# Dense products by column half, one cast behind each relu, row loads issued by GpSimd, and an early statistics record, in a three-layer graph network

## The chip, the cores and the metric

The kernel runs on one core of one Trainium2 chip. The metric is the device time of one execution in microseconds (us). PE is the matrix engine, DVE the vector engine, ACT the activation engine, POOL (GpSimd) issues indirect transfers, and SP issues most of the plain ones. ACT issues plain transfers too.

## The reference

A graph of 100,000 nodes with 128 values each and 25,000 edges, sorted by destination. The rows are normalised, three graph layers follow, each with a relu and a batch normalisation over all nodes, and the input is added.

```python
h = jnp.maximum(_layernorm(x, axis=-1), 0.0)
xn = _bn(h, g0, be0)
h = _bn(relu(_gcn_conv(xn, src, dst, edge_weight, W1, b1, n)), g1, be1)              # 128 -> 256
h = _bn(relu(_graph_conv(h, src, dst, edge_weight, Wrel2, brel2, Wroot2, n)), g2, be2)  # 256 -> 256
h = _bn(relu(_graph_conv(h, src, dst, edge_weight, Wrel3, brel3, Wroot3, n)), g3, be3)  # 256 -> 128
return x + h
# _graph_conv: segment_sum(ew[:, None] * x[src], dst) @ Wrel + brel + x @ Wroot
# _bn: g * (x - mean over all nodes) * rsqrt(var over all nodes + 1e-5) + b
```

## The kernel before

**Stages.** Setup, "norm", layers 1 to 3 (in the text l1, l2, l3) and "out", one behind the other, with a barrier between two. In a layer, two kinds of work share the engines. The *dense* work takes all nodes in 98 tiles of 1,024 columns (two column halves of 512), with channels on partitions. The *edge* work takes the edges in 49 chunks of 512, so two dense tiles go with one chunk. At a layer's end `fold` (line 1447) reads the batch statistics and folds scale and shift into the next weights. It aggregates, for each block of 128 channels, all 245 records that `bn_stats` left (two for each dense tile, one for each chunk), with one `bn_aggr` on DVE (line 1489). l1 and l2 have two blocks, l3 one.

**Dense work in l2 and l3** (`dense_layer`). Each f32 input is split: ACT casts it to a "top" part (`cast` in `tops`, line 1050), DVE subtracts that and leaves a "rest" part in place (`rests`, line 1078). PE then forms each product as three matmuls for each of two input blocks. A *unit* is one output block by one column half: 6 matmuls, then one relu on ACT (line 1037). A tile has `per` units, 4 in l2 and 2 in l3. Units alternate between two PSUM banks, so unit u+2 waits for the relu of unit u. Before a tile's first unit PE waits (`wait_use(pe, spl[j], i, kb * CH)`) until all four of its rests are done.

**What sets the order.** `pipeline` writes each engine's program as turns, one for each dense tile. A stage of lag L handles in turn t the tile t-L, so the lag says how many turns after its load a tile gets a step. The edge work has its steps in each second turn, ahead of the dense steps. I call the dense tile right behind edge work **A** and the next, which has no edge work ahead of it, **B**. A round is edge work, A, B. In l2 and l3 the dense stream starts slowly: its first 8 tiles come one in two turns, each right behind edge work. After these there are 45 rounds with an A and a B. The lags around the change are: casts and rests at `late` (8 tiles), products and relus at `ahead` = `late` + 2, and statistics one later. So before the change a tile's two halves are cast and split two turns ahead of its products.

**Edge work.** In l2 a chunk needs on ACT two relus of source rows (1371), two affines (1380), two copies of a product (1388), two "sum" casts (1415), and two casts of the destination inputs (`hd_top`, 1438, placed behind a dense tile's steps). In l2 DVE multiplies, scans (1309) and splits, and in l3 it multiplies and scans. The scan needs the chunk's same-node flags (`row_same`, 128 KB) and in l2 the weights (`row_weight`, 256 KB). ACT issues both transfers behind the affines (1351, 1353). POOL issues four gathers for each chunk (1170) once PE has turned the chunk two before.

## Time and profile before

| | us |
|---|---|
| median of 3 runs | 3771.5 (3755.3 to 3779.79) |
| the profiled execution, its own time | 3759.16 |
| its span in the trace | 3757.3 |
| PE busy | 2988.7 (80%) |
| DVE busy | 2613.1 (70%) |
| ACT busy | 2327.1 (62%) |
| POOL busy | 1348.4 (36%) |
| DMA, mean over the span | 304 GB/s |

The trace shows l1 until 1301 us, its fold until the first work of l2 at 1330, l2 until 2442, l3 from 2469 to 3219, and "out" behind it. A busy share is a mean over stages, so what bounds one stage is read from that stage's rows. The ends of matmuls are modelled: two matmuls that follow each other without a gap start 0.23 us apart although each is drawn 0.39 us long. So PE's lost time is read from the starts.

### The profile page before, as it was taken

What the parts mean: (1) busy time and instruction counts of PE and PEld (TensorE: products, weight loads), DVE (VectorE), ACT (ScalarE), POOL (GpSimd) and SP (SyncE); (2) the same over time, 40 slices, a digit from 0 to 9 for tenths busy, and PEclk for the clock granted to TensorE, in tenths of its full rate; (3) what the DMA queues carried; (4) which work ended last, traced back from release to release, by engine and by line L of the source; (5) the groups of instructions that cost most, each with busy time, mean ns of one, the idle gap of its engine ahead of it and who ended that gap; (6) DMA issues with size and microseconds to landing.
All of it is one profiled execution on the core that took longest, in us unless ns stands there. A gap on an engine that the chain in (4) does not pass through costs nothing. (4 is left out here: it accounts for less than half of the span.)

```text
span 3757.3 us, 52409 instructions
## 1 busy us (share of the span) xinstructions
PE 2988.7 (80%) x12445; PEld 2000.6 (53%) x12445; DVE 2613.1 (70%) x5586; ACT 2327.1 (62%) x4070; POOL 1348.4 (36%) x1194
## 2 busy tenths in 40 slices
PE   3565658988899769999999999959999999554543
PEld 3455534444444346777777777735555555333332
DVE  6576647877777858888888888757877777533332
ACT  4586736666666547877788778736666666333331
POOL 1444555545455232222222221022222321067475
PEclk9787879999999979999999999979999999655555
DMA  5586648888788769999999999769999999799997
GB/s 202 192 286 223 228 169 298 309 294 299 287 313 306 273 215 345 337 340 339 343 334 340 346 340 339 275 208 320 346 348 351 346 339 339 290 368 362 378 361 233
DMA packets 344639, 1142.11 MB, mean 304 GB/s; under 512 B 55625, under 2 KB 103266, under 8 KB 294386
## 3 DMA queue, kind: packets, MB, share of 16 engines
q1 hardware_dynamic: 221468, 933.98, 66.6%
q0 software_dynamic: 62656, 77.70, 12.2%
q10 hardware_dynamic: 60438, 129.60, 9.7%
q8 instruction: 24, 0.39, 0.0%
q14 instruction: 53, 0.43, 0.0%
HBM read 625.81 MB, written 515.28 MB: 304 GB/s over the span
## 5 line engine op out<-in xcount | busy, mean ns | idle before, releaser
L1170 POOL DMA_INDIRECT l_ed_gathered<-agg_rows,pos_cols x392 | 432.0, 1102 | 1462.7 <-PE l_ps L1182 704.0
L1078 DVE TENSOR_TENSOR l_dn_hi<-l_dn_hi,l_dn_top 128x512 fp32r<-128x512 f32 x784 | 501.5, 687 | 248.2 <-ACT l_dn_top L1050 228.0
L1023 PE MATMUL l_ps<-l_dn_top,wroot_top 128*128 128x512 f32 x1176 | 503.0, 428 | 85.9 <-ACT l_dn_ho L1037 43.3
L1037 ACT ACTIVATE l_dn_ho<-l_ps,bias_fold 128x512 f32<-128x512 f32 x588 | 395.8, 682 | 151.9 <-PE l_ps L1023 148.6
L1050 ACT ACTIVATE l_dn_top<-l_dn_hi 128x512 fp32r<-128x512 f32 x784 | 448.0, 623 | 65.2 <-DMA l_dn_hi<-h_dense 65.2
L1023 PE MATMUL l_ps<-l_dn_hi,wroot_top 128*128 128x512 f32 x1176 | 466.8, 397 | 0.0
L1023 PE MATMUL l_ps<-l_dn_top,wroot_rest 128*128 128x512 f32 x1176 | 466.4, 397 | 0.0
L685 PE MATMUL l_ps<-l_dn_columns,w_fold 128*128 128x512 f32 x784 | 391.3, 624 | 62.5 <-ACT l_dn_ho L720 55.6
L1608 POOL DMA_INDIRECT out<-out_rows_dst,out_cols x196 | 305.2, 1557 | 289.5 <-DMA out<-out_od_ot 189.6
L609 PE MATMUL norm_ln_ps<-norm_ln_ho 128*128 128x130 f32 x1568 | 248.3, 319 | 182.9 <-ACT norm_ln_ho L597 93.3
L597 ACT ACTIVATE norm_ln_ho<-norm_ln_x,norm_ln_nbias,norm_ln_rstd 128x128 f32<-128x128 f32 x784 | 303.8, 480 | 106.5 <-DVE norm_ln_nbias L550 102.8
L1067 DVE BATCH_NORM_STATS2 bn_stats_all<-l_dn_ho 128x512 f32 (+1 forms) x588 | 365.5, 678 | 2.0 <-ACT l_dn_ho L1037 2.0
L1629 PE MATMUL out_ps<-ident,out_od_hi 128*128 128x128 f32 x784 | 191.9, 426 | 189.6 <-ACT out_od_hi L1617 186.7
L609 PEld LDWEIGHTS norm_ln_ps<-norm_ln_ho 128*128 128x128 f32 x1568 | 228.1, 228 | 203.1 <-ACT norm_ln_ho L597 103.3
L1023 PEld LDWEIGHTS l_ps<-l_dn_top,wroot_top 128*128 128x128 f32 x1176 | 222.8, 189 | 201.1 <-issue 83.1
L798 POOL DMA_INDIRECT l_ed_src_rows<-h_rows,src_cols x196 | 213.0, 1087 | 310.8 <-PE l_ps L880 245.5
L720 ACT ACTIVATE l_dn_ho<-l_ps,bias_fold 128x512 f32<-128x512 f32 x392 | 261.4, 693 | 67.0 <-PE l_ps L685 42.4
L1645 DVE TENSOR_TENSOR out_od_ot<-out_ps,out_od_xt 128x512 f32<-128x512 f32 x196 | 135.5, 692 | 227.6 <-PE out_ps L1629 218.3
L639 POOL DMA_INDIRECT h_rows<-map_values,out_cols x196 | 190.2, 971 | 277.2 <-issue 202.1
L1629 PEld LDWEIGHTS out_ps<-ident,out_od_hi 128*128 128x128 f32 x784 | 153.1, 222 | 228.5 <-ACT out_od_hi L1617 169.8
L685 PEld LDWEIGHTS l_ps<-l_dn_columns,w_fold 128*128 128x128 f32 x784 | 135.8, 194 | 241.6 <-ACT l_dn_ho L720 146.3
L1617 ACT ACTIVATE out_od_hi<-out_od_hi,bn_shift,bn_scale 128x1024 f32<-128x1024 f32 x98 | 121.5, 1240 | 216.5 <-DMA out_od_hi<-h_dense 200.3
(233 smaller groups left out, 5900.2 us busy)
## 6 DMA issues: line engine op xcount, KB each, us to landing
h_dense<-l_dn_ho SPq DMA_DIRECT2D x196, 1024.0 KB, 10.2
l_dn_hi<-h_dense SPq DMA_DIRECT2D x196, 1024.0 KB
l_dn_rows<-h_rows SPq DMA_DIRECT2D x98, 520.0 KB
h_rows<-norm_ln_ho SPq DMA_DIRECT2D x97, 520.0 KB
h_dst<-l_ed_ho SPq DMA_DIRECT2D x98, 512.0 KB, 10.6
l_ed_hd<-h_dst ACTq DMA_DIRECT2D x98, 512.0 KB
h_dense<-l_dn_ho SPq DMA_DIRECT2D x98, 512.0 KB
out_od_hi<-h_dense SPq DMA_DIRECT2D x98, 512.0 KB
```

Source lines behind the costliest of these rows:

```text
L597: ins = act.activation(ho[:, j, g, 0:C], xt[:, j, g, :], ACT.Relu, bias=nb[:, j, g:g + 1], scale=rs[:, j, g:g + 1])
L609: ins = pe.matmul(ps[:, 0, 0:TC], ho[0:rows, j, g, 0:C], ho[0:rows, j, g, :], start=first and g == 0, stop=final and g == G - 1, skip_grou ...
L685: pe.matmul(ps[:, 2 + u % 2, 0:CW], wfold[1][:, 0, m * C:(m + 1) * C], hc[:, j % 2, c * CW:(c + 1) * CW], start=True, stop=True).then_inc( ...
L720: act.activation(ho[:, j, m, c * CW:(c + 1) * CW], ps[:, 2 + u % 2, 0:CW], ACT.Relu, bias=bfold[1][:, m:m + 1]).then_inc(rl[j], 1)
L1023: ins = pe.matmul(o, a, b, start=t == 0, stop=t == len(terms) - 1)
L1037: act.activation(ho[:, j, m, c * CW:(c + 1) * CW], ps[:, u % 2, 0:CW], ACT.Relu, bias=bf[:, m:m + 1]).then_inc(rl[j], 1)
L1050: act.activation(top[:, j % 2, k, cc], hi[:, j, k, cc], ACT.Copy).then_inc(tp[j], 1)
L1067: dve.bn_stats(stats[:, m, (i * NS + j) * CH + c, :], ho[:, j, m, c * CW:(c + 1) * CW]).then_inc(st[j], 1)
L1078: dve.tensor_tensor(rest[:, j, k, cc], hi[:, j, k, cc], top[:, j % 2, k, cc].bitcast(FP), ALU.subtract).then_inc(spl[j], 1)
L1170: pool.indirect_dma_start(tg[:, j, g, :], None, tab[n - 1][:, :], bass.IndirectOffsetOnAxis(ap=pos_c[:, t:t + 1], axis=0)).then_inc(gat[j] ...
L1608: pool.indirect_dma_start(out[:, :], bass.IndirectOffsetOnAxis(ap=out_c[0:rows, t:t + 1], axis=0), rows_dst[0:rows, t, :], None, compute_o ...
L1629: ins = pe.transpose(ps[0:P, bank0 + (j % 2) * banks + b, g * C:(g + 1) * C], hi[:, j, e:e + P], ident[:, :])
```

## The change

Five things change together.

1. In l2 and l3 the units of a tile go by column half first (`c, m = divmod(u, mb)`).
2. The casts are spread. The list of four is: second column half of the tile at `late + 1`, blocks 0 and 1, then first column half of the tile at `late`, blocks 0 and 1. In l2 one stands behind each relu, in l3 two. The rests follow their casts, `rests(1)` at lag `late + 1` and `rests(0)` at `late`. Products stay at `late + 2`.
3. In l2 the destination casts (`hd_top`) go from ACT to DVE, just ahead of their rests (`hd_parts`).
4. Flags and weights for the scan are issued by POOL instead of ACT: the first two chunks' at the start, the others' behind the gathers of two chunks later.
5. `first_groups`: at dense tile 92, DVE aggregates the records of the first 88 tiles (176 of the 245 records of each block) and writes one record in the place of the 176th. The fold aggregates the 70 that are left.

How the order moves. ACT in l2, in a round: before, then now (`l_dn_ho` is written by the relus, `l_dn_top` by the dense casts, `l_ed_hd_top` by the destination casts):

```order
L1388 ACTIVATE l_ed_rel<-l_ps 128x512 x2
L1037 ACTIVATE l_dn_ho<-l_ps,bias_fold 128x512 x3
L1050 ACTIVATE l_dn_top<-l_dn_hi 128x512 x2
L1037 ACTIVATE l_dn_ho<-l_ps,bias_fold 128x512
L1050 ACTIVATE l_dn_top<-l_dn_hi 128x512 x2
L1438 ACTIVATE l_ed_hd_top<-l_ed_hd 128x512 x2
L1037 ACTIVATE l_dn_ho<-l_ps,bias_fold 128x512 x3
```

```order
L1428 ACTIVATE l_ed_rel<-l_ps 128x512 x2
L1065 ACTIVATE l_dn_ho<-l_ps,bias_fold 128x512
L1077 ACTIVATE l_dn_top<-l_dn_hi 128x512
L1065 ACTIVATE l_dn_ho<-l_ps,bias_fold 128x512
L1077 ACTIVATE l_dn_top<-l_dn_hi 128x512
L1065 ACTIVATE l_dn_ho<-l_ps,bias_fold 128x512
L1077 ACTIVATE l_dn_top<-l_dn_hi 128x512
```

Between the relus of A and those of B stood four dense casts in pairs and two destination casts. Now one cast stands between two relus, and the pattern goes on through B.

ACT in l3, in the slow start, between the edge work (1380 or 1421 are the affines) and a tile's relus, before and now:

```order
L1371 ACTIVATE l_ed_ho_src<-l_ps,bias_fold 128x512 x2
L1345 DMA l_ed_hs<-h_src 128x1024
L1380 ACTIVATE l_ed_xa<-l_ed_ho_src,bn_shift,bn_scale 128x512 x2
L1351 DMA l_ed_same<-row_same 128x512
L1037 ACTIVATE l_dn_ho<-l_ps,bias_fold 128x512
L1050 ACTIVATE l_dn_top<-l_dn_hi 128x512 x2
```

```order
L1412 ACTIVATE l_ed_ho_src<-l_ps,bias_fold 128x512 x2
L1392 DMA l_ed_hs<-h_src 128x1024
L1421 ACTIVATE l_ed_xa<-l_ed_ho_src,bn_shift,bn_scale 128x512 x2
L1077 ACTIVATE l_dn_top<-l_dn_hi 128x512 x2
L1065 ACTIVATE l_dn_ho<-l_ps,bias_fold 128x512 x2
L1077 ACTIVATE l_dn_top<-l_dn_hi 128x512 x2
```

Two casts now stand between the affines and the relus. They are the second half of the very tile whose relus follow. The flags' transfer is gone from ACT.

DVE in l2, the last rounds (1067 or 1098 are the dense statistics, 1078 or 1109 the dense rests, 1428 or 1473 the destination rests), before and now:

```order
L1297 TENSOR_TENSOR l_ed_xa<-l_ed_xa,l_ed_coef 128x512 x2
L1309 SCALAR_TENSOR_TENSOR l_ed_sum<-l_ed_same,l_ed_sum,l_ed_xa 128x512 x2
L1067 BN_STATS bn_stats_all<-l_dn_ho 128x6 x4
L1078 TENSOR_TENSOR l_dn_hi<-l_dn_hi,l_dn_top 128x512 x4
L1428 TENSOR_TENSOR l_ed_hd<-l_ed_hd,l_ed_hd_top 128x512 x2
```

```order
L1344 TENSOR_TENSOR l_ed_xa<-l_ed_xa,l_ed_coef 128x512 x2
L1356 SCALAR_TENSOR_TENSOR l_ed_sum<-l_ed_same,l_ed_sum,l_ed_xa 128x512 x2
L660 BN_AGGR l_first_mv<-bn_stats_all 128x2 x2
L664 TENSOR_SCALAR bn_stats_all<-l_first_mv 128x2x2
L665 COPY bn_stats_all<-l_first_mv 128x2x2
L666 TENSOR_SCALAR bn_stats_all<-l_first_mv 128x2x2
L1098 BN_STATS bn_stats_all<-l_dn_ho 128x6 x4
L1109 TENSOR_TENSOR l_dn_hi<-l_dn_hi,l_dn_top 128x512 x4
L1470 CAST l_ed_hd_top<-l_ed_hd 128x512 x2
```

The early aggregation (once in a layer) stands ahead of statistics and rests of its turn, and two casts stand ahead of the destination rests in each round.

The diff:

```diff
--- before.py
+++ after.py
@@ -41,6 +41,7 @@
 PS = 125
+FIRST_TILES, AT_TILE = 88, 92
 RSQRT_SEED = 0x5f3759df
@@ -645,6 +646,29 @@
+        def first_groups(dve, ph, st, per, blocks):
...
+            G0 = FIRST_TILES * CH
+            s, mv = ph.sem("first_steps"), ph.sb("first_mv", [C, blocks, 2])
...
+            def aggregate():
+                for j in range(NS):
+                    dve.wait_ge(st[j], per * uses(NS, j, FIRST_TILES))
+                for b in range(blocks):
+                    dve.bn_aggr(mv[:, b, :], stats[:, b, 0:G0, :].rearrange("p g s -> p (g s)")).then_inc(s, 1)
+                dve.wait_ge(s, blocks)
+                one = stats[:, 0:blocks, G0 - 1, :].rearrange("p b (h s) -> p b h s", h=2)
+                wide = lambda n: mv[:, :, n:n + 1].broadcast_to([C, blocks, 2])
+                dve.tensor_scalar(one[:, :, :, 0], wide(0), 0.0, float(G0 * CW // 2), ALU.mult, ALU.add).then_inc(s, 1)
+                dve.tensor_copy(one[:, :, :, 1], wide(0)).then_inc(s, 1)
+                dve.tensor_scalar(one[:, :, :, 2], wide(1), float(G0 * CW // 2), None, ALU.mult).then_inc(s, 1)
+                dve.wait_ge(s, blocks + 3)
...
+            return aggregate
...
         def dense_rows(ph, ps):
@@ -733,7 +757,11 @@
+                aggregate = first_groups(dve, ph, st, per, 2)
...
                 def statistics(i, j):
+                    if isinstance(i, int) and i * NS + j == AT_TILE:
+                        aggregate()
                     for u in range(per):
@@ -1005,7 +1033,7 @@
                     for u in range(per):
-                        m, c = divmod(u, CH)
+                        c, m = divmod(u, mb)
@@ -1027,7 +1055,7 @@
                 def relu(u):
-                    m, c = divmod(u, CH)
+                    c, m = divmod(u, mb)
@@ -1039,29 +1067,32 @@
-                def tops(c):
-                    def cast(i, j):
-                        if c == 0:
+                def cast(c, k):
+                    def top_of(i, j):
+                        if c == 0 and k == 0:
                             wait_use(act, got[j], i, 16)
                         i2, j2 = before(i, j, 2, NS)
-                        wait_use(act, mm[j2], i2, per, per - CH + c + 1)
-                        for k in range(kb):
-                            cc = slice(c * CW, (c + 1) * CW)
-                            act.activation(top[:, j % 2, k, cc], hi[:, j, k, cc], ACT.Copy).then_inc(tp[j], 1)
...
-                    return cast
...
+                        wait_use(act, mm[j2], i2, per, (c + 1) * mb)
+                        cc = slice(c * CW, (c + 1) * CW)
+                        act.activation(top[:, j % 2, k, cc], hi[:, j, k, cc], ACT.Copy).then_inc(tp[j], 1)
...
+                    return top_of
...
+                casts = [(late + c, cast(c, k)) for c in (1, 0) for k in range(kb)] if split else []
                 stages = []
...
                     stages.append((ahead, relu(u)))
-                    if split and u >= per - CH:
-                        stages.append((late, tops(u - per + CH)))
+                    stages += casts[u * len(casts) // per:(u + 1) * len(casts) // per]
                 return NS, stages, None
...
             def vector(dve):
+                aggregate = first_groups(dve, ph, st, per, mb)
...
                 def statistics(i, j):
+                    if isinstance(i, int) and i * NS + j == AT_TILE:
+                        aggregate()
                     for u in range(per):
-                        m, c = divmod(u, CH)
+                        c, m = divmod(u, mb)
                         wait_use(dve, rl[j], i, per, u + 1)
@@ -1070,14 +1101,16 @@
-                def rests(i, j):
-                    for c in range(CH):
+                def rests(c):
+                    def half(i, j):
                         for k in range(kb):
...
-                return NS, [(ahead + 1, statistics)] + ([(late, rests)] if split else []), end
+                    return half
...
+                return NS, [(ahead + 1, statistics)] + ([(late + 1, rests(1)), (late, rests(0))] if split else []), end
@@ -1160,7 +1193,17 @@
             def gpsimd(pool):
+                def load_rows(k):
+                    i, j = divmod(k, slots)
+                    wait_use(pool, scn[j], i - 1, kb)
+                    pool.sem_inc(gate_l, 1)
+                    pool.dma_start(ss[:, j, :], line(r_same, k)).then_inc(in_b[j], 16)
+                    if n == 2:
+                        pool.dma_start(cf[:, j, :], line(r_ew, k)).then_inc(in_b[j], 16)
...
                 def end():
+                    for k in range(slots):
+                        load_rows(k)
                     for k in range(EC):
@@ -1169,6 +1212,10 @@
                                                     bass.IndirectOffsetOnAxis(ap=pos_c[:, t:t + 1], axis=0)).then_inc(gat[j], 16)
+                        if k >= 2 * slots:
+                            load_rows(k - slots)
+                    for k in range(EC - slots, EC):
+                        load_rows(k)
@@ -1346,12 +1393,6 @@
-                def load_rows(i, j):
-                    k = i * slots + j
-                    act.dma_start(ss[:, j, :], line(r_same, k)).then_inc(in_b[j], 16)
-                    if n == 2:
-                        act.dma_start(cf[:, j, :], line(r_ew, k)).then_inc(in_b[j], 16)
...
                 def load_dst(i, j):
@@ -1379,7 +1420,6 @@
                                        scale=sca[n - 1][:, k:k + 1]).then_inc(aff[j], 1)
-                    load_rows(i, j)
@@ -1422,25 +1462,20 @@
             def vector_parts(dve):
-                def hd_rest(i, j):
+                def hd_parts(i, j):
+                    i1, j1 = before(i, j, 1, slots)
+                    wait_use(dve, in_c[j], i, 32)
+                    wait_use(dve, mm_d[j1], i1, mb)
+                    for k in range(kb):
+                        dve.tensor_copy(d_top[:, k, :], hd_in[:, j, k, :]).then_inc(d_tp[j], 1)
                     for k in range(kb):
...
-                return slots, [(l_dst - 1, hd_rest)], None
...
-            def scalar_parts(act):
-                def hd_top(i, j):
-                    i1, j1 = before(i, j, 1, slots)
-                    wait_use(act, in_c[j], i, 32)
-                    wait_use(act, mm_d[j1], i1, mb)
-                    for k in range(kb):
-                        act.activation(d_top[:, k, :], hd_in[:, j, k, :], ACT.Copy).then_inc(d_tp[j], 1)
...
-                return slots, [(l_dst - 1, hd_top)], None
+                return slots, [(l_dst - 1, hd_parts)], None
...
             work = dict(sync=sync, gpsimd=gpsimd, tensor=tensor, vector=vector, scalar=scalar)
-            return (work, dict(vector=vector_parts, scalar=scalar_parts)) if n == 2 else work
+            return (work, dict(vector=vector_parts)) if n == 2 else work
@@ -1486,7 +1521,7 @@
                     for b in range(blocks):
-                        dve.bn_aggr(mv[:, b, :], stats[:, b, 0:groups, :].rearrange("p g s -> p (g s)")).then_inc(s, 1)
+                        dve.bn_aggr(mv[:, b, :], stats[:, b, FIRST_TILES * CH - 1:groups, :].rearrange("p g s -> p (g s)")).then_inc(s, 1)
                     done[0] += blocks
...
                     mean, var = mv[:, :, 0], mv[:, :, 1]
```

## Rows read from the trace of the kernel before

**Rows 1.** Stretches of l2 and l3: length, busy us of each engine, clock, DMA share, GB/s.
```profile
1500.00:2400.00 900.00, 864.43 (x3685) 636.51 (x3684) 759.52 (x1146) 720.35 (x1229) 180.14 (x149) 1.00 1.00 338
2600.00:3180.00 580.00, 577.75 (x2082) 338.59 (x2081) 460.10 (x708) 389.51 (x665) 156.19 (x152) 1.00 1.00 347
```
**Rows 2.** PE's timeline, a round of l2: start, duration, name, idle before and releaser.
```profile
2039.90 0.39 PE L1236 MATMUL l_ps<-l_ed_mask,ones_row 1*128 1x512 bf16 x1
...
2054.61 0.40 PE L1023 MATMUL l_ps<-l_dn_top,wroot_top 128*128 128x512 f32 x1
...
2058.42 0.50 PE L1023 MATMUL l_ps<-l_dn_top,wroot_top 128*128 128x512 f32 x1 [0.85 <-ACT l_dn_ho L1037]
...
2061.85 0.39 PE L1236 MATMUL l_ps<-l_ed_mask,ones_row 1*128 1x512 bf16 x1
```
**Rows 3.** ACT's timeline in the same round of l2.
```profile
2052.01 0.69 ACT L1037 ACTIVATE l_dn_ho<-l_ps,bias_fold 128x512 f32<-128x512 f32 x1 [0.63 <-PE l_ps L1023]
...
2056.65 1.15 ACT L1438 ACTIVATE l_ed_hd_top<-l_ed_hd 128x512 fp32r<-128x512 f32 x2
2057.69 1.26 ACT L1037 ACTIVATE l_dn_ho<-l_ps,bias_fold 128x512 f32<-128x512 f32 x2
```
**Rows 4.** DVE's timeline in the same round of l2.
```profile
2050.35 2.45 DVE L1067 BATCH_NORM_STATS2 bn_stats_all<-l_dn_ho 128x512 f32 x4
```
**Rows 5.** Groups of DVE instructions by form: count, busy us, mean ns, idle before.
```profile
L1525 DVE CAST wroot_top<-wroot_fold 128x512 fp32r<-128x512 f32 x1 | 0.4, 428 | 0.0
```
**Rows 6.** PE's timeline, a round of l3: the first matmul of B, and the next round.
```profile
2916.57 0.50 PE L1023 MATMUL l_ps<-l_dn_top,wroot_top 128*128 128x512 f32 x1
...
2919.79 0.38 PE L1236 MATMUL l_ps<-l_ed_mask,ones_row 1*128 1x512 bf16 x1
```
**Rows 7.** ACT's timeline in the same round of l3.
```profile
2915.84 0.67 ACT L1037 ACTIVATE l_dn_ho<-l_ps,bias_fold 128x512 f32<-128x512 f32 x1
2916.41 1.14 ACT L1050 ACTIVATE l_dn_top<-l_dn_hi 128x512 fp32r<-128x512 f32 x2
```
**Rows 8.** DVE's timeline in the same round of l3, and in the next.
```profile
2917.07 1.29 DVE L1078 TENSOR_TENSOR l_dn_hi<-l_dn_hi,l_dn_top 128x512 fp32r<-128x512 f32 x2 [1.49 <-ACT l_dn_top L1050]
...
2925.47 1.28 DVE L1297 TENSOR_TENSOR l_ed_xa<-l_ed_xa,l_ps 128x512 f32<-128x512 f32 x2
```
**Rows 9.** PE's timeline, end of l3.
```profile
3214.51 0.47 PE L1023 MATMUL l_ps<-l_dn_top,wroot_top 128*128 128x512 f32 x1 [0.25 <-DVE l_dn_hi L1078]
```
**Rows 10.** DVE's timeline, end of l3.
```profile
3213.11 1.29 DVE L1078 TENSOR_TENSOR l_dn_hi<-l_dn_hi,l_dn_top 128x512 fp32r<-128x512 f32 x2 [0.32 <-ACT l_dn_top L1050]
```
**Rows 11.** PE's timeline in the slow start of l2 and of l3.
```profile
1409.10 0.40 PE L1219 MATMUL l_ps<-l_ed_sum_top,wrel_rest 128*128 128x512 f32 x1
...
2507.24 0.58 PE L1236 MATMUL l_ps<-l_ed_mask,ones_row 1*128 1x512 bf16 x1 [6.72 <-DVE l_ed_sum L1309]
```
**Rows 12.** ACT's timeline in the slow start of l2 and of l3.
```profile
1410.30 1.06 ACT L1388 ACTIVATE l_ed_rel<-l_ps 128x512 f32<-128x512 f32 x2
...
2529.85 0.69 ACT L1371 ACTIVATE l_ed_ho_src<-l_ps,bias_fold 128x512 f32<-128x512 f32 x1 [1.41 <-PE l_ps L1203]
...
2531.14 0.80 ACT L1380 ACTIVATE l_ed_xa<-l_ed_ho_src,bn_shift,bn_scale 128x512 f32<-128x512 f32 x1
```
**Rows 13.** The folds' aggregation: count, min/median/max ns, first and last start.
```profile
L1489 DVE BATCH_NORM_AGGREGATE l_fold_mv<-bn_stats_all x5: 6731/6791/6792, 1301.0 to 3219.4; 128x2 f32<-128x1470 f32 x5
```
**Rows 14.** DMA issues by ACT: count, KB each, median us from issue to landing.
```profile
l_ed_same<-row_same ACTq DMA_DIRECT2D x98, 128.0 KB, 9.8
l_ed_coef<-row_weight ACTq DMA_DIRECT2D x49, 256.0 KB, 15.2
```
**Rows 15.** POOL's timeline: a chunk's last gather in l1, and in l3.
```profile
941.99 0.95 POOL L798 DMA_INDIRECT l_ed_dst_rows<-h_rows,dst_cols  x1 [0.30 <-issue]
...
2916.81 0.96 POOL L1170 DMA_INDIRECT l_ed_gathered<-agg_rows,pos_cols  x1 [0.30 <-issue]
```
**Rows 16.** DVE's timeline: the first instruction on what that gather in l1 brought.
```profile
949.06 0.17 DVE L922 TENSOR_TENSOR l_ed_coef<-l_ed_src_rows,l_ed_dst_rows 128x4 f32<-128x4 f32 x1 [8.33 <-DMA l_ed_dst_rows<-h_rows,dst_cols]
```

## The prediction

> **What bounds the kernel now.** I read the stretches first. In l2 PE is busy 864.43 of 900 us, in l3 577.75 of 580, at full clock [rows 1], and ACT (80%) and DVE (84%) are less busy. So in both layers an edit counts only by what it does to PE. The clock is not at issue.
>
> The drawn length of a matmul hides PE's waits, so I read starts. A dense matmul follows the one before after 0.233 us, a unit of six takes 1.40, a tile of l2 5.6, a tile of l3 2.8. In l2 a round takes 2061.85 - 2039.90 = 21.95 us. B begins at 2054.61 and its third unit should begin 12 x 0.233 = 2.80 later, at 2057.41. It begins at 2058.42: PE loses 1.01 us to a relu [rows 2]. ACT shows why: the two destination casts run at 2056.65, behind dense casts, and B's first relu starts at 2057.69 [rows 3], though its unit was done at 2056.0. Nothing else in the round holds PE.
>
> In l3 a round has no such place, but B starts at 2916.57 and takes 3.22 us to the next round at 2919.79 [rows 6], where 2 x 1.40 and the gap of 0.1 ahead of the edge work would be 2.90.
>
> The question for the change is then which of PE's waits goes and which one comes. The one that comes is `spl`: PE starts a tile only when all four of its rests are done.
>
> **Part by part.**
>
> *One cast behind each relu, destination casts on DVE, l2.* In A and B ACT has relu 0.57 + cast 0.52 (by distance of starts; 0.62 for a cast alone) for each unit of 1.40, so each relu starts when its unit ends. The wait of 1.01 us goes, if B is not held elsewhere. B's second half is cast behind A's first two relus. The second of these relus starts at 2052.01 [rows 3], its cast ends 0.57 + 0.62 later, at 2053.2, the rest on DVE (0.69) at 2053.95, and B may start at 2054.1, with 0.11 from the end of a rest to PE: in the one place where the trace shows PE waiting for a rest, the pair ends at 3213.11 + 1.29 = 3214.40 and PE starts at 3214.51 [rows 9, 10]. B needs it at 2054.61, so there is 0.5 us to spare. DVE has the statistics done at 2050.35 + 2.45 = 2052.80 [rows 4], and so is there ahead of the cast. It gets two more casts a round, by the same cast elsewhere 428 ns each, some 0.35 in a row [rows 5], less than on ACT (1.15 the pair, rows 3). Its work grows from 0.84 x 21.95 = 18.5 us [rows 1] to 19.3 in a round of 20.95. So -1.01 x 45 rounds = **-45**. Ends: 0 (DVE late) and -45 (PE has no other wait to lose).
>
> *The same in l3, A and B.* ACT has four casts and two relus in a tile as before, in the same pattern. What changes is whose casts. The pair behind A's first relu, which belonged to a tile two turns away, now belongs to B, and PE wants B one tile later. From rows: A's first relu starts at 2915.84 (held by the affines), the pair of casts at 2916.41 [rows 7], DVE's pair of rests at 2917.07, as soon as the first cast is there, and that ends at 2918.36 [rows 8]. With 0.11 PE starts B at 2918.47, where it now starts at 2916.57: +1.90. B then finds its relus done and takes 2.90 in place of 3.22: -0.32. So +1.58 a round, and I see nothing that could hide it, as PE has no slack in l3. It holds for the 41 rounds with edge work on both sides: +65. In the last few tiles, without edge work, DVE's six operations of 0.6 us already set 3.6 us a tile, and the new chain gives 3.7: +1. Together **+66**, ends 55 and 72.
>
> *The slow start.* There a tile comes right behind edge work, and now so do the casts of its own second half. In l3 PE ends the edge work some 0.2 us ahead of 2529.85, ACT's affines end at 2531.85 [rows 12], where its relu used to follow. From the start of a pair of casts to PE are 2918.47 - 2916.41 = 2.06 us (above), so PE starts at 2533.91 and not at 2529.65: +4.26. Eight tiles: +34. The chunk-0 flags now go out at the layer's start, and PE's wait of 6.72 us for the first scan [rows 11] goes: **+27**. In l2 the copies of the product are in the way: PE is done at 1409.10 + 0.23, the copies start at 1410.30 [rows 11, 12] and free ACT 0.95 later, at 1411.25, and PE starts at 1413.31, 4.0 late. About 1.0 comes back, since the wait for the relu is there too. Seven tiles: **+21**. Ends for both starts together: 0 if PE catches up on edge work it does not have, 60 if the first waits stay.
>
> *The early record.* An aggregation of 245 records takes 6.79 us [rows 13], so of 70 it takes 1.94 and of 176 4.88. The folds give back 5 x 4.85 = 24 us, all of it on the path, since all engines wait there. But DVE does 5 x 4.88 and nine small operations (2 us) more, at tile 92, ahead of the statistics and rests of its turn. In l2 B's second half is among these and has under 1 us of slack: 10.4 us are lost, 9.7 won, about 0. In l3 +5.5 against -4.85, as DVE sets the pace there. In l1 nothing is split. The last mask is a turn ahead and DVE has idle time, so I take half of 10.4 as paid: -4.5. Sum **-4**, ends -24 (all hidden) and +3.
>
> *Row loads by POOL.* ACT loses two issues a chunk in l2 and one in l3, which ran beside its affines: 0. POOL sits idle for most of a round. In l3 it issues the flags behind its last gather, 2916.81 + 0.96 + 0.30 = 2918.07 [rows 15]. DVE wants them at 2925.47 [rows 8], which moves on by 1.58 to 2927.05. For the landing the nearest rows are POOL's gather, 949.06 - 941.99 = 7.1 us [rows 15, 16], and the same transfer from ACT's queue, 9.8, with the weights at 15.2 [rows 14]. I take 7.1, since it has POOL's queue. It is in time. Up to 9.0 nothing waits, and up to 10.5 DVE makes it up from the 1.49 it waits for casts [rows 8]. In l2 a transfer has more than a round. **0**, the other end is the second rival.
>
> The Trainium skill, "DMA: Bandwidth & Descriptors" (Specifications; Issuing engine by pattern), has it the other way round: transfers from ACT or SP are generally faster, with the first byte after some 0.6 us against 1 us from GpSimd. By it the landing would be 9.8 + 0.4 = 10.2 us, and the sum would still be the same, 0.3 us short of where it starts to cost. This trace has POOL's gather sooner than ACT's load of flags, though the gather is smaller.
>
> **Sum.** -45 + 66 + 27 + 21 - 4 = +65 on the profiled execution's 3759.2, so 3824. The median of the runs stands 12.3 above that execution, so I forecast **3836**, 1.7% slower.
>
> **Rivals.**
>
> 1. *Not slower: B's rests don't hold PE in l3 or the starts.* The place is PE's wait for `spl` ahead of B. It decides at 2916.57: if DVE ends B's last rest 0.11 ahead of that, l3 keeps its 14.77 us a round. Then -45 - 4 are left, with l3's own -7: 3771.5 - 56 = 3715. For it: l2 has such a place and 0.5 us to spare. Against it: in l3 the rest ends at 2918.36, 1.9 us too late, and no engine could do these steps earlier in this order.
> 2. *Slower still: flags land late in l3.* If a landing from POOL takes 15.2 us, DVE's scans and then B's rests come late. Each round gets longer, which gives half of it back: (15.2 - 10.5) / 2 = 2.35 x 41 = 96 more, 3932. It decides at 10.5 us. The Trainium skill, "SBUF — State Buffer" (Who interferes with whom), adds a cause: a copy or cast on DVE in its fast mode keeps GpSimd from writing descriptors until it ends. By that the transfers in l2 could slip by the pair's 0.7 to 0.9 us, which has a round to go. No run here shows it.
> 3. *DVE becomes the bound of l2.* It waits for casts in each turn and has 0.5 us to spare ahead of B. If its two casts make it miss that, the 1.01 us turns into a wait for rests: +45, 3881.
> 4. *The starts cost little and the record is hidden.* Then -48 and -20 on the forecast: 3768, no change.
>
> **Chances.** Forecast 0.60, rivals in order 0.12, 0.08, 0.12, 0.08. A measurement of this kernel tells about 1% from no change, so "same" is 3734 to 3809. Rival 1 is faster, most of it: 0.10. Rival 4, the upper edge of rival 1 and the lower edge of the forecast (an early record that is better hidden, a cheaper start) are same: 0.20. The rest is slower: 0.70. Range: from 3780, which holds the forecast with the record hidden and half the starts, to 3888, which holds rival 3.
>
> **What would show it.** Right: in l2 rounds of 20.95 us and no wait of PE for a relu in B. In l3 rounds of 16.3 us, PE waiting 1.9 us for DVE's L1109 ahead of each B. In the slow starts a wait of 4 us for L1109 ahead of each tile. Aggregations of 4.9 and 1.9 us, the first followed by a wait of PE in l2. Landings of the flags from POOL's queue around 7 us and no wait of DVE for them. Wrong: rounds of l3 at 14.8 (rival 1) or above 17 with DVE waiting for flags (rival 2), rounds of l2 at 22 with PE waiting for rests (rival 3).

## The result, and the profile after

The changed kernel takes **3897.25 us** (median of 4 runs, 3882.05 to 3910.19) against 3763.4 of the kernel before on the same chip (median of 4, 3752.23 to 3779.79). The ratio is 1.035, 95% interval 1.031 to 1.039: slower, as forecast, but by 134 us and not by 65. It lies 61 us above the forecast 3836 and 9 us above the upper end of the range. The profiled execution has a span of 3897.3 us, 140.0 above the span before. (In experiment 1 below, one of four runs took 8033.9 us and is left out of its time and ratio.)

The two stretches of [rows 1], now (length, busy us of PE, PEld, DVE, ACT and POOL, granted clock of TensorE, DMA share, GB/s):

```profile
1500.00:2400.00 900.00, 895.77 (x3858) 672.04 (x3858) 815.69 (x1284) 725.45 (x1203) 238.52 (x242) 1.00 1.00 354
2600.00:3180.00 580.00, 512.97 (x1792) 309.46 (x1791) 402.99 (x610) 342.59 (x577) 155.75 (x170) 0.96 0.91 296
```

In l2 PE does 3858 matmuls where it did 3685, and in the rounds the profile shows no wait of PE. In l3 it does 1792 where it did 2082, and the granted clock is 0.96 where it was 1.00. DVE, at 91% of l2, doesn't set the pace.

To place the difference I count from fixed points: the folds, and PE's first mask matmul of an edge chunk (49 chunks a layer, numbered from 0).

| from, to | before | after | difference | forecast |
|---|---|---|---|---|
| start, fold of l1 | 1301.0 | 1318.9 | +17.9 | +5 |
| fold of l1, chunk 4 of l2 (fold, slow start) | 166.9 | 194.1 | +27.2 | +11 |
| chunk 4, chunk 46 of l2 (rounds) | 922.9 | 874.7 | -48.2 | -45 |
| chunk 46, fold of l2 (early record) | 51.4 | 61.6 | +10.3 | +10 |
| fold of l2, chunk 7 of l3 (fold, slow start) | 152.8 | 184.1 | +31.3 | +19 |
| chunk 7, chunk 47 of l3 (rounds) | 590.6 | 682.2 | +91.6 | +63 |
| chunk 47, fold of l3 (tail, early record) | 33.8 | 49.9 | +16.1 | +7 |
| fold of l3, end | 537.9 | 531.8 | -6.1 | -5 |
| sum | 3757.3 | 3897.3 | +140.0 | +65 |

The last column is the forecast's sum, laid out over the same points. The record's term lies partly in the stretches ahead of a fold (+5, +10, part of +7) and comes back in the folds (-9.7 in each of the first two, -4.9 in the last).

**l3.** PE's timeline of two rounds (start, duration, name, idle before it and releaser), to be read beside [rows 6]:

```profile
2914.11 0.80 PE L1051 MATMUL l_ps<-l_dn_top,wroot_top 128*128 128x512 f32 x1
...
2917.07 0.39 PE L1051 MATMUL l_ps<-l_dn_top,wroot_rest 128*128 128x512 f32 x1
2919.31 0.75 PE L1051 MATMUL l_ps<-l_dn_top,wroot_top 128*128 128x512 f32 x1 [1.85 <-DVE l_dn_hi L1109]
2919.86 0.63 PE L1051 MATMUL l_ps<-l_dn_hi,wroot_top 128*128 128x512 f32 x1
2920.29 0.63 PE L1051 MATMUL l_ps<-l_dn_top,wroot_rest 128*128 128x512 f32 x1
...
2922.84 0.39 PE L1051 MATMUL l_ps<-l_dn_top,wroot_rest 128*128 128x512 f32 x1
...
2923.86 0.39 PE L1283 MATMUL l_ps<-l_ed_mask,ones_row 1*128 1x512 bf16 x1
...
2935.03 0.40 PE L1051 MATMUL l_ps<-l_dn_top,wroot_rest 128*128 128x512 f32 x1
2937.34 0.49 PE L1051 MATMUL l_ps<-l_dn_top,wroot_top 128*128 128x512 f32 x1 [1.92 <-ACT l_dn_ho L1065]
2937.67 0.39 PE L1051 MATMUL l_ps<-l_dn_hi,wroot_top 128*128 128x512 f32 x1
...
2940.32 0.39 PE L1283 MATMUL l_ps<-l_ed_mask,ones_row 1*128 1x512 bf16 x1
```

Both B's wait 1.9 us, as forecast. The view names ACT for the second, but the relu that B's first unit needs, A's first, ended at 2934.69 + 0.67 = 2935.36. The rests decide there too: DVE ends B's last rest at 2935.91 + 1.29 = 2937.20, and PE starts at 2937.34. In the 40 rounds from chunk 7 this wait is 1.84 to 1.94 us long, and 2.62 in one. Behind the first wait the matmuls are 0.43 us apart and drawn 0.63 long until 2922.84: that is 1.2 GHz, half of the 2.4 GHz at which they are 0.233 apart. B takes 2923.86 - 2919.31 = 4.55 us, where the forecast had 2.90. Behind the second wait the clock stays up and B takes 2.98. Of the 40 rounds from chunk 7, 24 take 16.4 us (forecast 16.35) and 16 take 18.0.

ACT's and DVE's timelines of the first of these rounds, with A's first relu and B's rests of the second (compare [rows 7, 8]):

```profile
2916.75 0.66 ACT L1065 ACTIVATE l_dn_ho<-l_ps,bias_fold 128x512 f32<-128x512 f32 x1
2917.32 1.14 ACT L1077 ACTIVATE l_dn_top<-l_dn_hi 128x512 fp32r<-128x512 f32 x2
...
2934.69 0.67 ACT L1065 ACTIVATE l_dn_ho<-l_ps,bias_fold 128x512 f32<-128x512 f32 x1
```
```profile
2917.97 1.29 DVE L1109 TENSOR_TENSOR l_dn_hi<-l_dn_hi,l_dn_top 128x512 fp32r<-128x512 f32 x2 [1.55 <-ACT l_dn_top L1077]
...
2935.91 1.29 DVE L1109 TENSOR_TENSOR l_dn_hi<-l_dn_hi,l_dn_top 128x512 fp32r<-128x512 f32 x2 [1.49 <-ACT l_dn_top L1077]
```

The affines hold the relu, the relu the casts, the casts the rests: 2919.31 - 2917.32 = 1.99 us from the casts to PE, where I took 2.06.

**Slow start of l3.** PE's timeline in one tile of it, and DVE's rests of the tile's second half:

```profile
2560.58 0.47 PE L1051 MATMUL l_ps<-l_dn_top,wroot_top 128*128 128x512 f32 x1 [4.07 <-issue]
...
2561.66 0.63 PE L1051 MATMUL l_ps<-l_dn_top,wroot_top 128*128 128x512 f32 x1
...
2564.54 0.39 PE L1051 MATMUL l_ps<-l_dn_hi,wroot_top 128*128 128x512 f32 x1
...
2565.10 0.39 PE L1283 MATMUL l_ps<-l_ed_mask,ones_row 1*128 1x512 bf16 x1
```
```profile
2559.19 1.29 DVE L1109 TENSOR_TENSOR l_dn_hi<-l_dn_hi,l_dn_top 128x512 fp32r<-128x512 f32 x2 [0.98 <-ACT l_dn_top L1077]
```

The wait is 4.07 us (forecast 4.26). It ends with the rests, at 2559.19 + 1.29 = 2560.48, 0.10 ahead of PE. Then the tile takes 4.52 us and not the 2.9 of full clock, again by matmuls 0.43 apart. From chunk to chunk it is 17.35 us, where it was 11.49.

**Record, loads.** DVE's timeline at tile 92 of l2, PE's there, the folds' aggregations and the flags' issues in l3 with their landing:

```profile
2396.55 9.67 DVE L660 BATCH_NORM_AGGREGATE l_first_mv<-bn_stats_all 128x2 f32<-128x1056 f32 x2
```
```profile
2410.52 0.77 PE L1051 MATMUL l_ps<-l_dn_top,wroot_top 128*128 128x512 f32 x1 [10.19 <-issue]
```
```profile
L1524 DVE BATCH_NORM_AGGREGATE l_fold_mv<-bn_stats_all x5: 1992/2050/2050, 1318.9 to 3365.5; 128x2 f32<-128x420 f32 x5
```
```profile
L1200 POOL DMA_DIRECT2D l_ed_same<-row_same x29: 587/587/597, 2713.3 to 3192.3; - x29
...
who waited for it (us, times):
  DVE l_ed_xa L1344: 2.2, 1
...
DMA to landing us min/median/max: 7.3/7.8/8.7
```

The record costs PE a wait of 10.19 us in l2. The flags land after 7.8 us (I took 7.1, [rows 14] has 9.8 from ACT's queue), and DVE waited for them once in 29. In that round (chunk 20) POOL began its gathers later than in its neighbours and so issued the flags later. They landed after 8.6 us, DVE waited 2.2 us, and PE's wait ahead of B grew to 2.62. That is what the second rival describes, in this one round.

### The profile page after: what moved, and what is told of

Its sections match the earlier page's. It is cut to its first block and busy times, and to the rows that moved or that the text cites. A ratio compares the mean times of both kernels' runs of the same rounds, so it can differ in the third digit from the quotient of the medians.

```text
span 3897.3 us, 52378 instructions
## 1 busy us (share of the span) xinstructions
PE 3022.8 (78%) x12445; PEld 2041.9 (52%) x12445; DVE 2646.4 (68%) x5698; ACT 2301.1 (59%) x3972; POOL 1427.4 (37%) x1341
## 5 line engine op out<-in xcount | busy, mean ns | idle before, releaser
L1051 PE MATMUL l_ps<-l_dn_top,wroot_top 128*128 128x512 f32 x1176 | 513.4, 437 | 214.5 <-issue 114.2
L1065 ACT ACTIVATE l_dn_ho<-l_ps,bias_fold 128x512 f32<-128x512 f32 x588 | 403.5, 686 | 283.8 <-PE l_ps L1051 270.7
L1077 ACT ACTIVATE l_dn_top<-l_dn_hi 128x512 fp32r<-128x512 f32 x784 | 465.3, 620 | 50.6 <-DMA l_dn_hi<-h_dense 50.6
L1051 PE MATMUL l_ps<-l_dn_hi,wroot_top 128*128 128x512 f32 x1176 | 489.7, 416 | 0.0
L1051 PE MATMUL l_ps<-l_dn_top,wroot_rest 128*128 128x512 f32 x1176 | 487.8, 415 | 0.0
L1051 PEld LDWEIGHTS l_ps<-l_dn_top,wroot_top 128*128 128x128 f32 x1176 | 236.7, 201 | 309.1 <-issue 192.8
L826 POOL DMA_INDIRECT l_ed_src_rows<-h_rows,src_cols x196 | 211.3, 1078 | 327.6 <-PE l_ps L908 262.7
L744 ACT ACTIVATE l_dn_ho<-l_ps,bias_fold 128x512 f32<-128x512 f32 x392 | 261.6, 693 | 77.9 <-PE l_ps L709 47.2
L1051 PEld LDWEIGHTS l_ps<-l_dn_hi,wroot_top 128*128 128x128 f32 x1176 | 236.9, 201 | 63.8 <-issue 10.3
```

The source lines that it names most:

```text
L744: act.activation(ho[:, j, m, c * CW:(c + 1) * CW], ps[:, 2 + u % 2, 0:CW], ACT.Relu, bias=bfold[1][:, m:m + 1]).then_inc(rl[j], 1)
L1051: ins = pe.matmul(o, a, b, start=t == 0, stop=t == len(terms) - 1)
L1065: act.activation(ho[:, j, m, c * CW:(c + 1) * CW], ps[:, u % 2, 0:CW], ACT.Relu, bias=bf[:, m:m + 1]).then_inc(rl[j], 1)
L1077: act.activation(top[:, j % 2, k, cc], hi[:, j, k, cc], ACT.Copy).then_inc(tp[j], 1)
```

## The experiments

Nine kernels ran, in three sessions. Experiments 6 to 9 have one run each, so their totals carry little, and their traces are what is read. The kernel before took 3805.5 us beside the first four, 3627.4 beside the next three and 3755.5 beside the last two, so totals are compared only within a session. Rounds of l2 and l3 of the same code agree between the sessions to 0.02 us and are compared throughout. Rows are from the view of stretches: exactly 30 rounds, chunk 10 to chunk 40 of the layer, so that the length over 30 is the round. In it before and after show, l2 and then l3:

```profile
1600.40:2259.53 659.13, 633.53 (x2701) 466.25 (x2701) 557.33 (x841) 527.95 (x902) 145.20 (x120) 1.00 1.00 340
2639.23:3082.23 443.00, 441.36 (x1592) 258.76 (x1591) 350.92 (x541) 298.84 (x511) 122.92 (x120) 1.00 0.99 346
```
```profile
1637.94:2263.04 625.10, 625.10 (x2701) 468.76 (x2701) 569.36 (x901) 506.90 (x841) 180.19 (x180) 1.00 1.01 359
2684.16:3196.00 511.84, 454.56 (x1591) 274.64 (x1591) 357.01 (x541) 303.28 (x511) 137.32 (x150) 0.96 0.92 299
```

That is 21.97 and 14.77 us before, 20.84 and 17.06 after.

**1. The dense part put back** (the other edits stay).

```diff
-                        c, m = divmod(u, mb)
+                        m, c = divmod(u, CH)
...
-                casts = [(late + c, cast(c, k)) for c in (1, 0) for k in range(kb)] if split else []
...
-                    stages += casts[u * len(casts) // per:(u + 1) * len(casts) // per]
+                    if split and u >= per - CH:
+                        stages.append((late, tops(u - per + CH)))
...
-                return NS, [(ahead + 1, statistics)] + ([(late + 1, rests(1)), (late, rests(0))] if split else []), end
+                return NS, [(ahead + 1, statistics)] + ([(late, rests)] if split else []), end
```

> The changed kernel with the dense products, casts and rests of before (rows half by half of the blocks, both halves of a tile cast and split one turn after another tile's relus, no extra turn); destination tops by DVE, Pool's loads and the early record stay. Theory A (the second half's extra turn costs all that l3 and the slow starts lost): rounds of l3 back from 17.1 to 14.8 us (-94), both slow starts back (-40 and -27), low clock gone from l3. Within it two cases for l2: if taking the destination pair off ACT is what frees B's relu, l2 stays at 20.9 us a round and the time is about 3720; if it takes the spread casts, l2 is at 21.95 again and the time about 3765. Rival B (l3 lost its time to Pool's flags or to the destination work, not to the halves): l3 stays above 16 us a round and the time above 3830.

Measured: 3755.9 against 3805.5, ratio 0.987 (0.980 to 0.994). Its stretches of l2 and l3:

```profile
1638.10:2266.09 627.99, 627.99 (x2701) 466.59 (x2700) 566.23 (x901) 496.75 (x841) 153.60 (x180) 1.00 1.01 357
2636.37:3079.36 442.99, 441.42 (x1592) 258.77 (x1591) 353.81 (x541) 298.69 (x511) 148.47 (x149) 1.00 1.00 346
```

l3 is back at 14.77 us a round and clock 1.00, the slow starts too: fold of l1 to chunk 4 of l2 154.8 us, fold of l2 to chunk 7 of l3 141.5 (before 166.9 and 152.8, and the shorter aggregation takes 9.5 off each). Theory A holds, B falls. And l2 keeps 20.93 us: nearly the whole gain of l2 can be had without the halves and the spread casts.

**2. The halves' extra turn in l2 only.**

```diff
-                casts = [(late + c, cast(c, k)) for c in (1, 0) for k in range(kb)] if split else []
+                casts = [(late + c, cast(c, k)) for c in (1, 0) for k in range(kb)] if mb == 2 else [(late, cast(c, k)) for c in (0, 1) for k in range(kb)]
-                ... [(late + 1, rests(1)), (late, rests(0))] if split else []
+                ... [(late + 1, rests(1)), (late, rests(0))] if mb == 2 else [(late, rests(0)), (late, rests(1))]
```

> The changed kernel with the second half's extra turn in l2 only; in l3 casts and rests stand as before. Theory A: l3 rounds 14.8 us and its slow start back: 3897 - 94 - 40 = 3763, with l2 as in the changed kernel (20.9 us a round, slow start 27 us too long). Rival B: l3 stays above 16 us a round, above 3830.

Measured: 3786.7, ratio 0.993 (0.990 to 0.996). Rounds 20.84 in l2 and 14.77 in l3. Against experiment 1 it loses 31 us, and the trace shows the loss in l2's slow start: 193.4 us from the fold to chunk 4, against 154.8. For that it gains 0.1 us a round, 4 us over 42 rounds. So the halves (with the column-half order and the spread casts, which stay in l2) cost more at l2's start than they bring in its rounds.

**3. PE kept busy ahead of B in l3.** The fillers' result is overwritten by B's first unit.

```diff
+                    if mb == 1 and j % 2 == 0:
+                        i1, j1 = before(i, j, 1, NS)
+                        wait_use(pe, rl[j1], i1, per, per - 1)
+                        for f in range(12):
+                            pe.matmul(ps[:, 0, 0:kb * C], w_top[:, 0, 0:C], w_top[:, :, :].rearrange("p k c -> p (k c)"), start=True, stop=True)
                     if split:
                         wait_use(pe, spl[j], i, kb * CH)
```

> The changed kernel with 12 matmuls of 256 columns of weights against weights ahead of PE's wait for the rests of every second tile of l3 (B), into the bank that B's first unit starts anew: they change no result and keep PE busy for some 1.4 of the 1.9 us. Theory C (the 0.7 us a round beyond the forecast 16.35 are matmuls at 1.2 GHz, granted because PE stood still 1.9 us a round): granted clock of l3's rounds 1.00, rounds of 16.35 in place of 17.07, 3897 - 0.72 x 41 = 3868 or a little less. Rival D (0.7 us is in waits of its own, behind ACT or DVE): rounds stay at 17.1 or get longer by the fillers, 3897 or more.

Measured: 3908.3, ratio 1.028 (1.022 to 1.033), where the change itself has 1.035 (1.031 to 1.039). These intervals still overlap, so the reading rests on the rounds. Its stretch of l3, and PE's timeline ahead of a B:

```profile
2717.17:3208.87 491.70, 486.48 (x1951) 305.84 (x1951) 357.32 (x541) 302.04 (x511) 138.31 (x150) 1.00 0.93 312
```
```profile
2908.61 0.40 PE L1056 MATMUL l_ps<-l_dn_top,wroot_rest 128*128 128x512 f32 x1
2909.11 1.66 PE L1037 MATMUL l_ps<-wroot_top 128*128 128x256 f32 x12
2910.86 0.50 PE L1056 MATMUL l_ps<-l_dn_top,wroot_top 128*128 128x512 f32 x1
2911.20 0.39 PE L1056 MATMUL l_ps<-l_dn_hi,wroot_top 128*128 128x512 f32 x1
```

PE does 360 matmuls more and the 30 rounds are 20 us shorter: 16.39 us each, clock 1.00, none at 18. B starts as late as in the changed kernel, 2.25 us behind A's last matmul (there 2.24), and so it is the clock, not a further wait. Theory C is shown, D falls. From chunk 7 to chunk 47 it is 655.6 us against 682.2, 27 us less, or 0.67 a round.

**4. Destination tops on DVE, alone** (before, with `hd_top` moved as in the change and nothing else).

> The kernel before with one part of the change alone: the two destination tops of l2 on DVE, right ahead of their rests. My forecast put the whole 1.01 us a round down to the order of casts and relus with both edits together. Theory E (the pair of 1.15 us on ACT was all that held B's relu): the relu moves from 2057.69 to about 2056.6, rounds of l2 of 21.0, 3763 - 42 = 3721. Rival F (the relu is held by dense casts in a row): rounds of 21.9, 3763. Rival G (DVE is late with the pair, 0.85 us more in a row ahead of B's rests): above 21.95 a round, above 3763.

Measured: 3756.7, ratio 0.989 (0.986 to 0.992). Stretch of l2:

```profile
1609.63:2243.98 634.35, 632.75 (x2702) 465.09 (x2701) 566.31 (x901) 498.07 (x841) 119.17 (x120) 1.00 1.01 354
```

21.15 us a round, -0.83 of the -1.13 that the change has. Theory E holds, a little short of its 21.0. PE's time is not quite full: some rounds take 20.9 and more of them 21.3.

**5. Experiment 1 without the early record** (each fold aggregates all records, `0:groups`).

> The dense products, casts and rests of before, destination tops by DVE, Pool's loads, and no early record: each fold aggregates all 245 records again. Theory H (the record pays back in the folds what it takes where PE waits for DVE): the stretch from l1's 44th chunk to its fold 9 us shorter than with the record (70.9), from l2's 44th to its fold 9.5 shorter (100.7), l3's 5 shorter (83.4), against 5 x 4.85 = 24 us more in folds: no difference, 3756 on a chip where before takes 3805. Rival I (the record is a net gain of 10 us or more): above 3766. It is also the version to beat both kernels: l2 at 20.9 us a round, l3 at 14.8.

Measured: 3572.1 against 3627.4, ratio 0.985 (0.982 to 0.988), 55 us faster than before. Rounds of 20.92 and 14.77 us:

```profile
1451.27:2078.79 627.52, 627.52 (x2702) 466.57 (x2701) 566.36 (x901) 496.97 (x841) 154.19 (x180) 1.00 1.01 357
```

From chunk 44 to the fold it is 59.6, 90.9 and 77.6 us in the three layers, with the record (experiment 1) 70.9, 100.8 and 83.4. In l2 and l3 the record costs 9.9 and 5.8 us. l1 scatters: over all traces here 65.9 to 71.9 with the record, 59.6 to 64.7 without, 7 us between the means. 7 + 9.9 + 5.8 = 22.7 against 9.5 + 9.5 + 4.7 = 23.7 in the folds. Theory H holds: it pays for itself and no more. The ratios of experiments 1 and 5 can't be told apart.

**6. Fillers in the slow starts too.** As experiment 3, and:

```diff
+                    slow = isinstance(i, int) and i * NS + j < late
+                    fill = (16 if mb == 2 else 30) if slow else 12 if mb == 1 and j % 2 == 0 else 0
```

> As the kernel with fillers in l3, and also 30 matmuls of 256 columns ahead of the wait for rests of each of the first 8 tiles of l3, and 16 of 512 columns ahead of those of l2. Theory C (the slow starts cost more than forecast by matmuls at 1.2 GHz behind a wait of 4 us, 9 of 12 in a tile of l3): a tile of l3's slow start 15.7 us in place of 17.35, of l2's about 20 to 21 in place of 22.3. Rival D (it is the wait alone): 17.35 and 22.3 as in the changed kernel, or longer by fillers.

Measured: 3713.1 in one run, before 3627.4, so 2.4% above. Four intervals of l3's slow start, of this kernel and of the changed one:

```profile
2358.10:2421.88 63.78, 61.99 (x287) 40.79 (x285) 32.34 (x48) 27.91 (x45) 19.16 (x20) 1.00 0.69 219
```
```profile
2512.62:2582.76 70.14, 53.84 (x166) 30.29 (x165) 32.33 (x48) 27.87 (x45) 19.12 (x20) 0.90 0.64 203
```

A tile takes 15.79 us where it took 17.35, with the clock at 1.00 where it was 0.90. In l2 it is 20.18 against 21.6 to 22.7. Fold to chunk 4 of l2 is 9.7 us shorter, fold to chunk 7 of l3 10.7 us. (Between traces with the same order these stretches differ by up to 2 us: for l3, 184.1 in the changed kernel and 182.5 and 182.7 in experiments 9 and 8, once their folds are taken 9.5 shorter.) Theory C holds in the starts as well. What is left over before is the waits: 15.79 - 11.49 = 4.30 a tile in l3 (forecast 4.26), 20.18 - 16.15 = 4.03 in l2 (forecast 3.0).

**7. Pool's loads, alone** (before, with flags and weights issued by POOL as in the change).

> The kernel before with Pool issuing the flags and weights, and nothing else of the change. Forecast on record: 0. With destination tops on DVE, rounds of l2 took 21.14 us without and 20.93 with Pool's loads (and the early record, which is outside of them). Theory J (two issues a chunk on ACT's queue delay casts and relus of l2 by 0.2 us a round): rounds of l2 at 21.7 in place of 21.95, l3 at 14.77 as before. Rival K (they matter only with the destination pair gone): 21.95.

Measured: 3624.5 in one run, before 3627.4. Stretches of l2 and l3:

```profile
1470.37:2128.86 658.49, 632.89 (x2701) 466.50 (x2700) 557.30 (x841) 525.03 (x901) 180.19 (x180) 1.00 1.00 341
2504.98:2947.98 443.00, 441.40 (x1591) 258.81 (x1591) 351.89 (x541) 298.77 (x511) 155.66 (x150) 1.00 1.00 346
```

21.95 and 14.77: nothing, as forecast. But experiments 4 and 5 differ in these loads alone, and there they are worth 21.15 - 20.92 = 0.23 us a round. So rival K holds: they bring something only once the destination pair is gone from ACT. One thing was not forecast: in this order of steps DVE waits for the flags in each of the 30 rounds of l3, 40.1 us in all, and PE's round stays at 14.77. They land after 8.3 us (median).

**8. The dense part, alone** (before, with units by column half, spread casts and the extra turn).

> The kernel before with the dense part of the change alone: units by column half, one cast behind each relu, the second half cast and split a turn later; destination tops stay on ACT, flags and weights on ACT's queue, no early record. Theory E (the destination pair on ACT holds B's relu wherever the dense casts stand): rounds of l2 between 21.5 and 22. Rival F (spreading the casts frees the relu by itself): 20.9 to 21.1. Both: l3 rounds of 16.4, or 18 where the clock is low, the slow starts as in the changed kernel (22.3 and 17.35 us a tile).

Measured: 3909.2 in one run, before 3755.5: 154 us slower. l2 and l3:

```profile
1638.83:2275.42 636.59, 633.22 (x2702) 466.58 (x2701) 551.92 (x841) 533.50 (x901) 144.97 (x120) 1.00 1.01 352
2695.22:3208.24 513.02, 456.41 (x1592) 275.99 (x1591) 356.48 (x541) 303.61 (x511) 119.17 (x120) 0.96 0.92 300
```

21.22 us in l2, between the ranges of the two theories and in neither, nearer to F. Spreading the casts frees the relu nearly by itself, -0.75, and so does moving the pair, -0.83. Both remove the same wait, so they don't add up. l3 takes 17.10 us a round, and a tile of the slow starts 21.7 to 22.8 us in l2 and 17.1 to 17.2 in l3, as forecast. The whole loss of the change is in this part: alone it costs 154 us, the others together bring some 50 (experiment 1). These make 104 and the change measures 134, in good part because the gain in l2's rounds, some 35 us, is counted in both.

**9. The change without the early record.**

> The changed kernel without the early record. From l3's 47th chunk to its fold before took 33.8 us, the changed kernel 49.9, the old casts with the record 39.1. Theory L (record and late halves add up there): 44 to 45 us. Rival M (the record costs more where the rests have no slack): 40 or less. From l2's 44th chunk to its fold: 92 to 93 in place of 102.9. Rounds of l2 20.84, of l3 16.4 or 18 as in the changed kernel.

Measured: 3890.2 in one run, before 3755.5, ratio 1.036 as with the record. l3 from chunk 47 to the fold: 43.4 us (33.8 before, 49.9 with the record). l2 from chunk 44 to the fold: 90.6 (102.9 with it). Rounds of l2 and l3 are those of the changed kernel, 20.84 and 17.05. The two tails come out a little below the forecast (44 to 45, and 92 to 93), l3 nearer to theory L than to M: record and late halves add up, 6.5 and 9.6 us in l3's tail. In this kernel the record costs 12.3 us in l2 and 6.5 in l3, more than the 9.9 and 5.8 of experiment 5.

## Why the forecast had the direction and half of the size

**Right, with its numbers.** *Cast behind each relu, destination casts on DVE, l2*: forecast -1.01 us a round, measured -1.13, and PE is busy throughout. *A and B in l3*: a wait of 1.84 to 1.94 us ahead of 39 of 40 B's, 16.4 us a round in the rounds at full clock, forecast 1.90 and 16.35. *The slow start of l3*: 4.07 to 4.30 us a tile, forecast 4.26, and of PE's first wait of 6.72 a part is gone (the fold of l2 to chunk 7 of l3 takes 148.2 us in experiment 5 and 152.8 before). *Row loads*: 0 by themselves (experiment 7). But once the destination pair is gone they are worth 0.23 us a round of l2 (experiments 4 and 5), and how much of the -1.13 is theirs in the changed kernel no run shows. So that -1.13 comes near -1.01 is in part luck. *Early record*: net -4 forecast, about -1 with the old casts (experiment 5), and 7 + 12.3 + 6.5 - 23.7 = about +2 in the changed kernel (experiment 9). "Half of 10.4 paid" in l1 was too low, about 7 were paid.

**Wrong: each of these waits was priced as a wait alone.** The step that failed is the sentence that the clock is not at issue. It was read from [rows 1], at a granted clock of 1.00, and carried over to a kernel in which PE stands still in each round. In 16 of 40 rounds of l3 the matmuls behind the wait ran at 1.2 GHz. Of the 28 us that the rounds cost above their term, 27 go away with fillers (experiment 3). In the two slow starts 9.7 and 10.7 us go away (experiment 6), of the 16 and 12 that they cost above forecast, give or take the 2 us by which traces differ. These 47 us are nearly two thirds of the 75 that the traces show above the sum.

**Mis-sized besides.** (1) *The slow start of l2*: I took 1.0 of 4.0 us a tile as coming back, and 4.03 stayed: in six or seven tiles about 6 us, which is what experiment 6 leaves there. (2) *The tail of l3*: "+1" was 9.6 us (experiment 9 against before). The part of DVE's and PE's timelines that shows it:

```profile
3321.17 1.27 DVE L1344 TENSOR_TENSOR l_ed_xa<-l_ed_xa,l_ps 128x512 f32<-128x512 f32 x2
3322.36 2.45 DVE L1356 TENSOR_TENSOR_SCAN l_ed_sum<-l_ed_same,l_ed_sum,l_ed_xa 128x512 f32<-128x512 bf16 x2
...
3325.90 2.48 DVE L1109 TENSOR_TENSOR l_dn_hi<-l_dn_hi,l_dn_top 128x512 fp32r<-128x512 f32 x4
```
```profile
3327.28 0.77 PE L1051 MATMUL l_ps<-l_dn_top,wroot_top 128*128 128x512 f32 x1 [4.88 <-issue]
3327.84 0.63 PE L1051 MATMUL l_ps<-l_dn_hi,wroot_top 128*128 128x512 f32 x1
```

Ahead of the last chunk PE has no source work left, but DVE still has a chunk's product and scan (3.6 us) ahead of B's rests. So B waits 4.88 us and then runs at the lower clock. (3) l1 took 13 us more than its forecast of 5. The record explains about 2 of them (7 in place of 5). Its rounds (chunks 8 to 44), in which no edit changes anything, took 580 us before, 591 after, 595 to 621 in experiments 1 to 4, 555 to 564 in 5 to 7, 580 to 583 in 8 and 9. That is scatter and no part of the change. Where in it the median run of either kernel lies stays open.

**The rivals.** Rival 1 (B's rests don't hold PE) is refuted at its own point, the wait ahead of each B. Rival 2: the flags land after 7.8 us and not above 10.5, one wait of DVE in 29 issues. The Trainium skill, "SBUF — State Buffer" (Who interferes with whom), gave it a further cause; no landing here is long enough to need one, with 8.9 us the longest of l3. By the Trainium skill's "DMA: Bandwidth & Descriptors" (Issuing engine by pattern) ACT's queue is generally the faster one. In l2 the same transfer lands after 9.8 us (median) when ACT issues it and after 7.3 when POOL does, so the measurement decides. Rival 3: PE waits for nothing in l2 at DVE's 91%. Rival 4: the starts cost 37 and 41 us (27.2 and 31.3, with the 9.5 that each fold gives back) and the record is not hidden. None of them was the clock, and the range's upper end held no case for it.

**What beats both.** Experiment 5: destination tops on DVE, flags and weights by POOL, everything else as before. 0.985 of the time before (0.982 to 0.988). Experiments 1 and 4 also beat the kernel before, by 1.3 and 1.1%.

## What to carry to other kernels

A wait of PE has two prices: its length, and the matmuls behind it at half clock. Here 1.9 us cost 1.58 by itself and 0.67 more on average. When a change brings a new wait to a PE that was busy nearly all the time, give the clock a term of its own and put it into the range.

Look for the smallest edit that removes a wait: either of two edits freed the relu, and the one that left the order of the rests alone cost nothing. And price an edit in every layer that shares its code: what pays 0.75 us a round in l2, where a tile has slack, cost 2.3 in l3.

## What was not expected of the hardware

- Nearly the same pause, 1.84 to 1.94 us, was followed by a stretch at 1.2 GHz in some rounds (12 of the 30 of the stretch shown) and not in the others. The length of the pause doesn't tell them apart, and what does stays open. With 12 matmuls of 256 columns in the pause it was 0 of 30. A pause of 4 us in the slow start of l3 lowered it in the tile shown; its four intervals have a mean clock of 0.90. In the kernel before, PE waited some 0.85 us in each round of l2, and the granted clock there was 1.00 [rows 1, 2].
- The kernel before took 3627.4, 3755.5, 3763.4 and 3805.5 us in four sessions, up to 5% apart. Yet rounds of l3 without a wait took 14.76 to 14.77 us in the three of them that had such a kernel traced. The difference is ahead of l2: the traces of the fastest session reach l1's first chunk at 425 to 427 us, those of the others at 530 to 541.
- Two DMA issues a chunk on ACT's queue cost nothing beside the old order and 0.23 us a round of l2 once ACT had room. The traces don't show through which wait; that stays open.
